# A graph-attention layer on one core: h turned by DMA, v's lo halves behind the second masks, the raise on VectorE, a written-out closing

## The chip, the cores and the metric

The kernel runs on one core of one Trainium2 chip. The metric is the device time in microseconds of that core. Before the change three runs took 616.78, 616.84 and 617.56 us, median 616.84.

## What is computed

x is 32 batches of 256 tokens by 384 features, and adj is a boolean mask of 256 by 256 for each batch. Cut to what matters, the reference is:

```python
h = maximum(layernorm(x), 0.0)
q, k, v = heads(h @ Wq + bq), heads(h @ Wk + bk), heads(h @ Wv + bv)   # 6 heads of 64
scores = einsum('bhqd,bhkd->bhqk', q, k) / sqrt(64)
probs = softmax(scores + where(adj, 0.0, -9e15))
ctx = einsum('bhqk,bhkd->bhqd', probs, v)
out = x + ctx.reshape(32, 256, 384) @ Wf + bf
```

Inputs and outputs are float32. The kernel multiplies in float16 with each operand split into a high and a low half, so that most products are three matmuls: hi by hi, hi by lo, lo by hi.

## The kernel before, in words

Names: B is 32 batches, P is 128, S is 256 tokens in QT = 2 tiles t, C is 3 chunks of 128 features. A unit u (0 to 5) of a batch is a pair of heads j = u % 3 for one query tile t = u // 3. Every engine has its own program, written out by hand, in which the order of the work is fixed; engines meet only at semaphores. All of them go through `cycle(b)` for b = 1 to 33, and `cycle(b)` works on four batches at once: scores and softmax of batch b, the last four units of batch b-1 and its output, the output's second half of batch b-2, and the projections of batch b+1.

For each batch: VectorE takes the moments of x (`layer_stats`, `layer_moments`), GpSimd makes `normed` (`normalise`, L345). TensorE turns `normed` in six float32 transposes (`transpose_h`, L862, matmuls of L874) into PSUM banks ring 0 and ring 1; ScalarE writes the relu of it as `h_hi` (L486), VectorE the rest as `h_lo` (L637). TensorE projects q and k for each pair of heads (`project_qk`, 18 matmuls of 256 columns each) and v for each token tile (`project_v`, 9 matmuls of 384 columns each). ScalarE takes q and k out of PSUM (`qk_full`), VectorE and GpSimd split them; ScalarE writes `v_hi` (L500), VectorE `v_lo` (`v_lo_part`, L650).

`scores(b, g)` (L910) computes two units with 12 matmuls. `mask_and_max(b, u)` (L623) on VectorE adds the mask to the two heads of a unit and keeps the smallest element of each row in `least`; each head is one long instruction and one short one that reads the accumulator out. `exps` (L471) on ScalarE first adds a constant to `least`, giving `raised` (L475), and then takes two exponentials; `probs_hi` on ScalarE and `probs_lo` on GpSimd (L379) split them into `p_rows`. SyncE's queue turns `p_rows` into `p_cols` with one transposing DMA per unit (`transpose_probs`, L271). `apply_probs` (L927) multiplies by v into the bank ctx with 12 matmuls, four units after the scores. `divide` (L657) on VectorE needs three applied units. `transpose_context` (L944, three transposes), `context_hi`, `context_lo` and `project_out` (L955, 9 matmuls of 384 columns) make the output tile, `finish` (L672) adds the residual, and SyncE stores it.

Four PSUM banks are shared as a ring. Bank ring 3 holds v of tile 0 (`R_V[0]`, L154), then the output of tile 1 (`R_OUT[1]`, L156), then q and k of pair 1. So `project_out(b-2, 1)` of `cycle(b)` may overwrite ring 3 only when VectorE has read v of batch b out of it. It says so in its second wait (L957 and L958):

```python
def project_out(b, t):
    wait(pe, ct_lo_ready, b.count(2, t + 1))
    if t == 1 and (b + 2).exists():
        wait(pe, v_lo_ready, (b + 2).count(2, 1))
```

The start of `cycle(b)` before the change is, on TensorE (L1026 to L1034): scores(b, 0), apply_probs(b-1, 2), transpose_h(b+1), project_out(b-2, 1), apply_probs(b-1, 3), project_qk(b+1, 0), scores(b, 1). On VectorE (L803 to L817): mask_and_max(b, 0), divide(b-1, 0), h_lo_part(b+1), mask_and_max(b, 1), v_lo_part(b, 1), finish(b-2, 1). v_lo_part(b, 0) stands at the end of `cycle(b-1)` (L849).

Of the kernel before, what the change touches and what calls it, by code (L numbers as in the profile page):

```python
# [35 lines left out]
P = 128  # L36
# [17 lines left out]
def gnn_attention(nc, x, adj, Wq, bq, Wk, bk, Wv, bv, Wf, bf, out):  # L54
# [11 lines left out]
    with ctx:  # L66
# [23 lines left out]
        p_raise = sb("p_raise", [P, 1], F32)  # L90
# [28 lines left out]
        h_hi = [sb(f"h_hi{p}", [P, C, S], F16) for p in range(2)]  # L119
        h_lo = [sb(f"h_lo{p}", [P, C, S], F16) for p in range(2)]  # L120
# [36 lines left out]
        ctx_ps = ctx_bank[:, 0:HEADS * V1].rearrange("p (h d) -> p h d", h=HEADS)  # L157
# [35 lines left out]
        h_lo_ready = sem("h_lo_ready")  # L193
        qk_ready = sem("qk_ready")
# [11 lines left out]
        p_lo_ready = sem("p_lo_ready")  # L206
        ctx_ready = sem("ctx_ready")
# [32 lines left out]

        def pair(j):

            return slice(j * P, (j + 1) * P)
# [3 lines left out]

        def cycles(cycle):

            for k in range(1, B + 2):  # L250
                cycle(Batch(k))
# [8 lines left out]
        def _(sp):  # L260
# [10 lines left out]
            def transpose_probs(b, u):  # L271
# [3 lines left out]
                                       p_rows[u][:].rearrange("p w a k -> p (w a k)")).then_inc(p_placed[u], 16)  # L275

# [21 lines left out]
            def cycle(b):  # L298
# [20 lines left out]

                if here:  # L320
                    transpose_probs(b, 2)
# [14 lines left out]
            transpose_probs(Batch(0), 3)  # L336
            cycles(cycle)
            for t in range(QT):
                sp.wait_ge(out_stored[t], 16 * (B + 1))
# [3 lines left out]
        def _(pool):  # L343
            def normalise(b):
# [4 lines left out]
                wait(pool, ht_ready, b.count(2, 0))  # L349
# [35 lines left out]
            pool.memset(p_raise[:], P_RAISE).then_inc(pool_const, 1)  # L385
            pool.wait_ge(pool_const, 4)
# [80 lines left out]


        @block.scalar
        def _(act):  # L470
            def exps(b, u):  # L471

                wait(act, p_lo_ready, b.count(UNITS, u - 2))
                wait(act, logits_ready, b.count(2 * UNITS, 2 * u + 2))
                act.activation(raised[u % 3][:], least[u % 3][:], ACT.Identity,  # L475
                               bias=p_raise[:, 0:1]).then_inc(raised_ready, 1)
# [9 lines left out]
            def h_hi_part(b):  # L486
                for n, (c0, c1, src) in enumerate(((0, 2, R_HT[0]), (2, 3, R_HT[1]))):
                    wait(act, ht_ready, b.count(2, n + 1))
                    act.activation(h_hi[b.parity][:, c0:c1].rearrange("p c s -> p (c s)"),  # L489
                                   src[:, 0:(c1 - c0) * S], ACT.Relu).then_inc(h_hi_ready, 1)  # L490

# [32 lines left out]
            act.wait_ge(pool_const, 5)  # L524
# [33 lines left out]
            qk_full(Batch(1), 2)  # L558
            exps(Batch(0), 4)
# [50 lines left out]


# [473 lines left out]
```

## Time and profile before

| | |
|---|---|
| median of three runs | 616.84 us |
| profiled execution, its own time | 617.89 us |
| its span, first to last instruction | 616.0 us |
| mean granted TensorE clock | 0.989 |
| instructions | 18008 |

The profile is of one execution. Its own time is 1.89 us more than its span, and 1.05 us more than the median. Busy time of an engine is the sum over its instructions; matmuls overlap one another in this profile (their ends are modelled), so the distance from one start to the next tells what a matmul costs in a stream.

### The profile page before, as it was taken

The page shows a single profiled execution, that of the slowest core. Times are in us where ns is not written, and L with a number is a line of the kernel's source. Part 1 is how long each engine was busy: PE and PEld are TensorE (multiplying, and loading weights), DVE is VectorE, ACT ScalarE, POOL GpSimd, SP SyncE. Part 2 cuts the span into 40 slices and gives each one's busy share as a digit, 9 for nine tenths or more (in the row PEclk, how much of TensorE's full clock was granted, in tenths as well). Part 3 has the DMA queues.
Part 4 walks back from the last instruction along what each step waited for, and adds up shares of the span by engine and source line. Part 5 has one row for each costly group of instructions (what it writes and reads, how often), then busy time and mean ns, then how long its engine had stood idle before and what let it go on. Part 6 is the DMA issues. An engine that isn't in the chain of part 4 may idle for free.

```text
span 616.0 us, 18008 instructions
## 1 busy us (share of the span) xinstructions
PE 596.3 (97%) x6806; PEld 451.9 (73%) x6806; DVE 456.9 (74%) x1479; ACT 516.5 (84%) x1166; POOL 496.1 (81%) x529
## 2 busy tenths in 40 slices
PE   7998999999999999999999999999999999999975
PEld 7666777777777777777777777777777777777753
DVE  5878777878777777877777787777778777776762
ACT  2688888889888889988888898888889888888980
POOL 2789888888888888888888888888888888888750
PEclk9998999999999999999999999999999999999997
DMA  8056766867766786666578767666886666765573
GB/s 264 6 100 117 133 124 128 157 128 146 139 139 122 129 159 127 145 131 150 118 129 159 130 141 134 142 123 129 159 136 136 140 141 121 126 133 112 100 136 80
DMA packets 232280, 81.14 MB, mean 132 GB/s; under 512 B 214273, under 2 KB 232194, under 8 KB 232194
## 3 DMA queue, kind: packets, MB, share of 16 engines
q1 hardware_dynamic: 230992, 79.99, 66.1%
q8 instruction: 54, 0.88, 0.6%
q14 instruction: 32, 0.26, 0.2%
q10 hardware_dynamic: 1202, 0.01, 0.1%
HBM read 17.05 MB, written 12.58 MB: 48 GB/s over the span
## 4 chain that ended last, share of the span: by engine, by line
PE 87%; ACT 6%; DVE 2%; DMA 2%; issue 1%; POOL 1%; ACTq 0%; DVEq 0%; POOLq 0%
PE ring L858 19%; PE ring L860 19%; PE ring L859 19%; PE scores L922 11%; PE ctx L939 5%; PE ring L951 4%; PE ctx L940 3%; PE ctx L941 3%; PE ring L874 3%; ACT probs L479 2%; DMA bf_row<-in_L_gnn_bf_dram 1%; ACT qk L496 1%; ACT p_rows L484 1%; DMA p_cols<-p_rows 1%; PE ring L981 1%
## 5 line engine op out<-in xcount | busy, mean ns | idle before, releaser
L379 POOL TENSOR_TENSOR p_rows<-probs,p_rows 128x512 f16<-128x512 f32 x192 | 222.4, 1158 | 58.5 <-ACT p_rows L484 57.3
L632 DVE CUSTOM_DVE_ANT_0 logits<-scores,mask,logit_unscale 128x256 f32<-128x256 f32 x384 | 169.1, 477 | 39.0 <-PE scores L922 37.1
L479 ACT ACTIVATE probs<-logits,raised 128x256 f32<-128x256 f32 x384 | 174.3, 500 | 6.2
L858 PE MATMUL ring<-h_hi,w_hi 128*128 128x256 f16 x576 | 157.7, 274 | 0.6 <-DVE h_lo L640 0.6
L860 PE MATMUL ring<-h_hi,w_lo 128*128 128x256 f16 x576 | 157.5, 273 | 0.0
L859 PE MATMUL ring<-h_lo,w_hi 128*128 128x256 f16 x576 | 157.4, 273 | 0.0
L365 POOL TENSOR_TENSOR split<-qk,split 128x512 f16<-128x512 f32 x96 | 111.0, 1157 | 25.2 <-DVE split L648 25.2
L484 ACT ACTIVATE p_rows<-probs 128x512 f16<-128x512 f32 x192 | 121.0, 630 | 6.1
L496 ACT ACTIVATE qk<-ring,qk_bias_s,qkv_ratio 128x256 f32<-128x256 f32 x192 | 96.3, 551 | 3.9 <-PE ring L860 3.9
L939 PE MATMUL ctx<-v_hi,p_cols 128*128 128x65 f16 x768 | 90.7, 196 | 7.4 <-DMA p_cols<-p_rows 4.4
L939 PEld LDWEIGHTS ctx<-v_hi,p_cols 128*128 128x128 f16 x768 | 70.2, 97 | 33.4 <-issue 23.6
L652 DVE SCALAR_TENSOR_TENSOR v_lo<-ring,qkv_ratio,v_hi 128x384 f16<-128x384 f32 x64 | 39.5, 618 | 70.6 <-ACT v_hi L502 70.6
L940 PE MATMUL ctx<-v_lo,p_cols 128*128 128x64 f16 x768 | 90.1, 193 | 0.0
L941 PE MATMUL ctx<-v_hi,p_cols 128*128 128x65 f16 x768 | 89.7, 194 | 0.0
L922 PE MATMUL scores<-split 64*128 64x256 f16 x1152 | 80.2, 272 | 3.1 <-DVE least L632 2.2
L940 PEld LDWEIGHTS ctx<-v_lo,p_cols 128*128 128x128 f16 x768 | 71.2, 99 | 4.2
L922 PEld LDWEIGHTS scores<-split 64*128 64x128 f16 x1152 | 48.8, 94 | 31.2 <-issue 24.7
L941 PEld LDWEIGHTS ctx<-v_hi,p_cols 128*128 128x128 f16 x768 | 71.5, 98 | 0.0
L374 POOL TENSOR_TENSOR residual<-x_in,bf_full 128x384 f32<-128x384 f32 x64 | 68.3, 1087 | 0.0
L648 DVE CAST split<-qk 128x512 f16<-128x512 f32 x96 | 55.6, 579 | 14.1 <-ACT qk L496 12.1
L489 ACT ACTIVATE h_hi<-ring 128x512 f16<-128x512 f32 x64 | 27.9, 487 | 45.0 <-PE ring L874 45.0
L858 PE MATMUL ring<-w_hi,ct_hi 128*128 128x384 f16 x192 | 63.3, 329 | 1.7 <-DVE ct_lo L668 1.7
(89 smaller groups left out, 1222.2 us busy)
## 6 DMA issues: line engine op xcount, KB each, us to landing
x_in<-in_x_dram SPq DMA_DIRECT2D x32, 384.0 KB, 3.9
out_dram<-result SPq DMA_DIRECT2D x64, 192.0 KB, 2.2
p_cols<-p_rows SPq DMA_TRANSPOSE x192, 3.1
adj_in<-in_adj_dram SPq DMA_DIRECT2D x32, 64.0 KB, 2.6
w_raw<-in_L_gnn_Wq_dram SPq DMA_DIRECT2D x1, 576.0 KB, 5.8
w_raw<-in_L_gnn_Wv_dram SPq DMA_DIRECT2D x1, 576.0 KB, 7.9
w_raw<-in_L_gnn_Wf_dram SPq DMA_DIRECT2D x1, 576.0 KB, 9.1
w_raw<-in_L_gnn_Wk_dram SPq DMA_DIRECT2D x1, 384.0 KB, 6.8
```

The lines of the kernel that those rows point to most:

```text
L365: pool.tensor_tensor(split[b.parity][j][:, 0:4:3, :], qk32[j][:], split[b.parity][j][:, 1:3, :], ALU.subtract).then_inc(qk_lo_ready, 1)
L379: pool.tensor_tensor(p_rows[u][:, 1], probs[u % 3][:], p_rows[u][:, 0], ALU.subtract).then_inc(p_lo_ready, 1)
L479: act.activation(probs[u % 3][:, a], logits[u % 3][:, a], ACT.Exp, bias=raised[u % 3][:, a:a + 1], scale=-1.0).then_inc(probs_ready, 1)
L484: act.activation(p_rows[u][:, 0], probs[u % 3][:], ACT.Copy).then_inc(p_hi_ready, 1)
L632: dve.tensor_tensor_reduce(out=logits[u % 3][:, a], in0=score_bank[a][:, u % 2 * S:(u % 2 + 1) * S], in1=mask[b.parity][:, t], scale=logit ...
L858: pe.matmul(out_ap, a_hi, m_hi, start=first, stop=False)
L859: pe.matmul(out_ap, a_hi, m_lo, start=False, stop=False)
L860: return pe.matmul(out_ap, a_lo, m_hi, start=False, stop=last)
L922: mm = pe.matmul(score_bank[a][:, u % 2 * S:(u % 2 + 1) * S], tile[own, q, t * P:(t + 1) * P], tile[own, k], start=(n == 0), stop=(n == 2))
L939: pe.matmul(ctx_ps[:, h], hi, vh, start=(s == 0), stop=False)
L940: pe.matmul(ctx_ps[:, h, 0:D], hi, vl, start=False, stop=False)
L941: mm = pe.matmul(ctx_ps[:, h], lo, vh, start=False, stop=(s == QT - 1))
```

## The change

It has these parts.

- Batches 2 to 31: `normed` is no longer turned by TensorE. ScalarE writes its relu in float16 as it lies (`h_hi_rows`, two instructions), VectorE the rest (`h_lo_rows`, two instructions), and one transposing DMA of SyncE's queue per batch turns both halves into `h_cols`. In `cycle(b)` this is done for batch b+2. Batches 0 and 1 stay with TensorE. The waits by which ring 0 and ring 1 were kept for those transposes move to `project_qk`.
- v_lo_part(b, 0) moves from the end of `cycle(b-1)` to `cycle(b)`, behind mask_and_max(b, 1) and directly ahead of v_lo_part(b, 1). `project_out` is not changed.
- `raised` is made by VectorE at the end of every mask_and_max, after a wait for its own `least`, instead of by ScalarE.
- The cycles end with b = 30. What cycles 31 to 33 did is written out for every engine: units 4 and 5 of the last batch are turned by TensorE, the last batch's first context goes to the bank peaks, its second tile is divided, turned and projected in two parts (four heads, two heads), and its result is written to `normed`.

The diff, cut to its core:

```diff
+
+        h_rows = sb("h_rows", [P, 2, C, QT, P], F16)
+        h_cols = [sb(f"h_cols{p}", [P, 2, C, S], F16) for p in range(2)]
...
+        LAST, PREV = Batch(B - 1), Batch(B - 2)
+        last_pt = {4: ring[2], 5: score_bank[0]}
+        UP_TO, FROM = slice(0, 2), slice(2, 3)
+
+        def ctx_of(b, t):
+
+            bank = peak_bank if b.k == B - 1 and t == 0 else ctx_bank
+            return bank[:, 0:HEADS * V1].rearrange("p (h d) -> p h d", h=HEADS)
...
+        BY_PE = 2
+
         def cycles(cycle):
 
-            for k in range(1, B + 2):
+            for k in range(1, B - 1):
                 cycle(Batch(k))
...
+            def transpose_h(b):
+
+                wait(sp, h_lo_ready, b.count(2, 2))
+                sp.dma_start_transpose(h_cols[b.parity][:].rearrange("p w c (t k) -> p (w c t) k", k=P),
+                                       h_rows[:].rearrange("p w c t n -> p (w c t n)")).then_inc(h_placed, 16)
...
+                if (b + 2).exists():
+                    transpose_h(b + 2)
                 if here:
                     transpose_probs(b, 2)
...
+            transpose_h(Batch(2))
             cycles(cycle)
...
-                wait(pool, ht_ready, b.count(2, 0))
+                wait(pool, ht_ready if b.k <= BY_PE else h_lo_ready, b.count(2, 0))
...
+            probs_lo(PREV, 5)
+            probs_lo(LAST, 0)
+            probs_lo(LAST, 1)
+            probs_lo(LAST, 2)
+            probs_lo(LAST, 3)
...
                 wait(act, p_lo_ready, b.count(UNITS, u - 2))
-                wait(act, logits_ready, b.count(2 * UNITS, 2 * u + 2))
-                act.activation(raised[u % 3][:], least[u % 3][:], ACT.Identity,
-                               bias=p_raise[:, 0:1]).then_inc(raised_ready, 1)
                 wait(act, raised_ready, b.count(UNITS, u + 1))
                 for a in range(2):
...
+            def h_hi_rows(b):
+
+                wait(act, h_placed, (b.k - BY_PE) * 16)
+                for t in range(QT):
+                    wait(act, norm_ready, b.count(2, t + 1))
+                    act.activation(h_rows[:, 0, :, t], normed[:, t].rearrange("p (c n) -> p c n", n=P),
+                                   ACT.Relu).then_inc(h_hi_ready, 1)
...
-                if front:
-                    h_hi_part(b + 1)
...
+                if (b + 2).exists():
+                    h_hi_rows(b + 2)
                 if before:
...
+            def turned_hi(u, nth):
+
+                act.wait_ge(pt_ready, nth)
+                act.activation(p_cols[u][:, 0].rearrange("p a s q -> p (a s q)"), last_pt[u][:],
+                               ACT.Copy).then_inc(pt_hi_ready, 1)
...
+            exps(LAST, 0)
+            probs_hi(LAST, 0)
+            v_hi_part(LAST, 1)
+            exps(LAST, 1)
+            probs_hi(LAST, 1)
+            exps(LAST, 2)
+            probs_hi(LAST, 2)
+            context_hi(PREV, 0)
+            exps(LAST, 3)
+            probs_hi(LAST, 3)
+            exps(LAST, 4)
+            exps(LAST, 5)
+            turned_hi(4, 1)
+            context_hi(PREV, 1)
+            turned_hi(5, 2)
+            context_hi(LAST, 0)
+            context_hi_last(UP_TO, 2)
+            context_hi_last(FROM, 3)
...
+                dve.wait_ge(logits_ready, b.count(2 * UNITS, 2 * u + 2))
+                dve.tensor_scalar(raised[u % 3][:], least[u % 3][:], P_RAISE, None, ALU.add).then_inc(raised_ready, 1)
...
+            def h_lo_rows(b):
+
+                for t in range(QT):
+                    wait(dve, h_hi_ready, b.count(2, t + 1))
+                    dve.scalar_tensor_tensor(
+                        out=h_rows[:, 1, :, t], in0=normed[:, t].rearrange("p (c n) -> p c n", n=P),
+                        scalar=0.0, in1=h_rows[:, 0, :, t], op0=ALU.max, op1=ALU.subtract).then_inc(h_lo_ready, 1)
...
+            h_lo_rows(Batch(2))
             layer_stats(Batch(3), (1,))
             layer_moments(Batch(3))
-            v_lo_part(Batch(1), 0)
...
-                if front:
-                    h_lo_part(b + 1)
 
                 if here:
                     mask_and_max(b, 1)
                 if here:
+                    v_lo_part(b, 0)
                     v_lo_part(b, 1)
...
+                if (b + 2).exists():
+                    h_lo_rows(b + 2)
...
                     finish(b + -1, 0)
                     context_lo(b + -1, 1)
-                if front:
-                    v_lo_part(b + 1, 0)
 
             cycles(cycle)
...
+            def turned_lo(u, nth):
+
+                dve.wait_ge(pt_hi_ready, nth)
+                dve.tensor_tensor(p_cols[u][:, 1].rearrange("p a s q -> p (a s q)"), last_pt[u][:],
+                                  p_cols[u][:, 0].rearrange("p a s q -> p (a s q)"),
+                                  ALU.subtract).then_inc(pt_lo_ready, 1)
...
+            def divide_last(chunks, units, nth):
+
+                h = slice(2 * chunks.start, 2 * chunks.stop)
+                ctx_ps = ctx_of(LAST, 1)
+                dve.wait_ge(ctx_ready, LAST.count(UNITS, units))
+                dve.reciprocal(inv_sum[1][:, h], ctx_ps[:, h, D]).then_inc(inv_ready, 1)
+                dve.wait_ge(inv_ready, LAST.count(2, nth))
+                dve.tensor_tensor(context[1][:, h], ctx_ps[:, h, 0:D],
+                                  inv_sum[1][:, h].unsqueeze(2).to_broadcast([P, h.stop - h.start, D]),
...
+            mask_and_max(LAST, 0)
+            mask_and_max(LAST, 1)
+            divide(PREV, 0)
+            v_lo_part(LAST, 0)
+            v_lo_part(LAST, 1)
+            mask_and_max(LAST, 2)
+            mask_and_max(LAST, 3)
+            finish(PREV + -1, 1)
+            context_lo(PREV, 0)
+            mask_and_max(LAST, 4)
+            mask_and_max(LAST, 5)
+            divide(PREV, 1)
+            finish(PREV, 0)
+            turned_lo(4, 1)
+            context_lo(PREV, 1)
+            divide(LAST, 0)
+            turned_lo(5, 2)
+            finish(PREV, 1)
+            divide_last(UP_TO, 5, 2)
+            context_lo(LAST, 0)
+            context_lo_last(UP_TO, 2)
+            divide_last(FROM, 6, 3)
+            context_lo_last(FROM, 3)
+            finish_last(0)
+            finish_last(1)
 
 
...
-                    if (b + -3).exists():
-                        if n == 0:
-                            wait(pe, ct_lo_ready, (b + -3).count(2, 2))
-                        else:
-                            wait(pe, result_ready, (b + -3).count(2, 1))
...
-                if j == 0:
+                if j == 0 and b.k < BY_PE:
                     wait(pe, h_lo_ready, b.count(2, 2))
+                elif j == 0:
+                    wait(pe, h_placed, (b.k - BY_PE + 1) * 16)
+                if j == 0 and (b + -3).exists():
+                    wait(pe, ct_lo_ready, (b + -3).count(2, 2))
...
-                wait(pe, p_placed[u], b.count(16, 16))
+                ctx_ps = ctx_of(b, t)
+                if b.k == B - 1 and u >= 4:
+                    pe.wait_ge(pt_lo_ready, u - 3)
+                else:
+                    wait(pe, p_placed[u], b.count(16, 16))
                 if u == 0:
                     wait(pe, v_lo_ready, b.count(2, 2))
-                if j == 0:
+                if b.k == B - 1 and u == C:
+                    pe.wait_ge(context_ready, b.count(2, 0))
+                elif j == 0 and b.k != B - 1:
...
                 attend(0)
-                if front:
-                    transpose_h(b + 1)
                 if (b + -2).exists():
                     project_out(b + -2, 1)
...
+            def turn_probs(u):
+
+                if u == 4:
+                    pe.wait_ge(v_lo_ready, LAST.count(2, 2))
+                else:
+                    pe.wait_ge(logits_ready, LAST.count(2 * UNITS, 2 * UNITS))
+                for a in range(2):
+                    pe.wait_ge(probs_ready, LAST.count(2 * UNITS, 2 * u + a + 1))
+                    for n in range(QT):
+                        o = (a * QT + n) * P
+                        mm = pe.transpose(last_pt[u][:, o:o + P], probs[u % 3][:, a, n * P:(n + 1) * P], ident[:])
+                mm.then_inc(pt_ready, 1)
...
+            scores(LAST, 0)
+            apply_probs(PREV, 2)
+            project_out(PREV + -1, 1)
+            apply_probs(PREV, 3)
+            scores(LAST, 1)
+            transpose_context(PREV, 0)
+            apply_probs(PREV, 4)
+            scores(LAST, 2)
+            apply_probs(PREV, 5)
+            project_out(PREV, 0)
+            apply_probs(LAST, 0)
+            transpose_context(PREV, 1)
+            turn_probs(4)
+            apply_probs(LAST, 1)
+            turn_probs(5)
+            apply_probs(LAST, 2)
+            project_out(PREV, 1)
+            transpose_context(LAST, 0)
+            apply_probs(LAST, 3)
+            apply_probs(LAST, 4)
+            transpose_context_last(UP_TO, 2)
+            apply_probs(LAST, 5)
+            project_out(LAST, 0)
+            project_out_last(UP_TO, 2)
+            transpose_context_last(FROM, 3)
+            project_out_last(FROM, 3)
```

## Rows read from the trace of the kernel before

**Rows 1.** The page: busy time (share of the span) and instructions of the engines
```profile
PE 596.3 (97%) x6806; PEld 451.9 (73%) x6806; DVE 456.9 (74%) x1479; ACT 516.5 (84%) x1166; POOL 496.1 (81%) x529
```

**Rows 2.** The page: the chain that ended last, by engine
```profile
PE 87%; ACT 6%; DVE 2%; DMA 2%; issue 1%; POOL 1%; ACTq 0%; DVEq 0%; POOLq 0%
```

**Rows 3.** The chain in order of time, one cycle in the middle: start us, us, what
```profile
298.99 0.76 PE scores L922 x12
...
300.21 0.69 PE ring L874 x6
...
301.06 0.16 PE ring L859
...
316.91 0.76 PE scores L922 x12
```

**Rows 4.** Instructions of PE in time, start of that cycle: start us, us, what
```profile
298.92 0.83 PE L922 MATMUL scores<-split 64*128 64x256 f16 x12
...
300.02 0.20 PE L941 MATMUL ctx<-v_hi,p_cols 128*128 128x65 f16 x1
...
300.74 0.33 PE L858 MATMUL ring<-w_hi,ct_hi 128*128 128x384 f16 x1
...
304.63 0.83 PE L922 MATMUL scores<-split 64*128 64x256 f16 x12
```

**Rows 5.** Instructions of DVE in time, same cycle; in brackets idle time and its releaser
```profile
299.37 0.62 DVE L652 SCALAR_TENSOR_TENSOR v_lo<-ring,qkv_ratio,v_hi 128x384 f16<-128x384 f32 x1 [1.64 <-ACT v_hi L502]
299.90 0.47 DVE L632 CUSTOM_DVE_ANT_0 logits<-scores,mask,logit_unscale 128x256 f32<-128x256 f32 x1
...
300.71 0.08 DVE L632 DVE_READ_ACCUMULATOR2_ANT least<- 128x1 f32 x1
300.71 0.19 DVE L660 RECIPROCAL inv_sum<-ctx 128x6 f32<-128x6 f32 x1
300.93 0.56 DVE L662 TENSOR_TENSOR context<-ctx,inv_sum 128x384 f32<-128x384 f32 x1
301.41 1.01 DVE L640 SCALAR_TENSOR_TENSOR h_lo<-ring,h_hi 128x512 f16<-128x512 f32 x2
...
305.50 0.48 DVE L632 CUSTOM_DVE_ANT_0 logits<-scores,mask,logit_unscale 128x256 f32<-128x256 f32 x1 [0.48 <-PE scores L922]
```

**Rows 6.** Groups of instructions by form: busy us, mean ns | idle before
```profile
L697 DVE TENSOR_SCALAR neg_mean<-mean_var 128x2 f32<-128x2 f32 x32 | 5.8, 180 | 0.1
```

**Rows 7.** Busy time in stretches; behind POOL's: granted clock, DMA share, GB/s
```profile
45.50:48.40 2.90, 0.00 (x0) 0.03 (x1) 2.23 (x8) 2.87 (x7) 2.90 (x3) 1.00 0.43 82
50.20:53.60 3.40, 3.40 (x23) 1.97 (x21) 2.90 (x2) 2.80 (x7) 3.40 (x5) 0.50 0.68 93
53.60:57.00 3.40, 3.40 (x50) 3.06 (x49) 2.92 (x11) 2.30 (x6) 2.71 (x4) 1.00 0.85 200
600.90:603.80 2.90, 0.00 (x0) 0.00 (x0) 0.26 (x1) 0.00 (x0) 0.18 (x1) 0.89 1.12 155
603.20:610.00 6.80, 5.64 (x39) 3.81 (x39) 1.57 (x4) 0.49 (x1) 0.00 (x0) 0.50 0.19 50
591.90:593.70 1.80, 0.00 (x0) 0.00 (x0) 1.58 (x8) 1.74 (x6) 1.15 (x1) 1.00 0.97 216
```

**Rows 8.** The chain in order of time, the end: start us, us, what
```profile
598.94 4.86 DMA p_cols<-p_rows
...
607.37 0.32 PE ring L860
...
613.04 0.62 DVE result L677
```

**Rows 9.** Instructions of PE in time: the last batch's first scores
```profile
585.80 0.83 PE L922 MATMUL scores<-split 64*128 64x256 f16 x12
```

**Rows 10.** The page: DMA queues and issues (KB each where known, us to landing)
```profile
q1 hardware_dynamic: 230992, 79.99, 66.1%
...
p_cols<-p_rows SPq DMA_TRANSPOSE x192, 3.1
```

More of the change, by code:

```diff
@@ L206, in gnn_attention @@
         p_lo_ready = sem("p_lo_ready")
+        pt_ready = sem("pt_ready")
+        pt_hi_ready = sem("pt_hi_ready")
+        pt_lo_ready = sem("pt_lo_ready")
         ctx_ready = sem("ctx_ready")
@@ L336, in _, with store_last @@
             transpose_probs(Batch(0), 3)
+            transpose_h(Batch(2))
             cycles(cycle)
+            def store_last(t):
+                sp.wait_ge(result_ready, LAST.count(2, t + 1))
+                sp.dma_start(out_v[LAST.k, t], normed[:, t]).then_inc(out_stored[t], 16)
+            transpose_probs(PREV, 4)
+            store(PREV + -1, 0)
+            transpose_probs(PREV, 5)
+            transpose_probs(LAST, 0)
+            store(PREV + -1, 1)
+            for u in (1, 2, 3):
+                transpose_probs(LAST, u)
+            store(PREV, 0)
+            store(PREV, 1)
+            store_last(0)
+            store_last(1)
             for t in range(QT):
@@ L558, in _ @@
             qk_full(Batch(1), 2)
+            h_hi_rows(Batch(2))
             exps(Batch(0), 4)
@@ new lines, in context_lo_last, with finish_last @@
+            def context_lo_last(chunks, nth):
+                dve.wait_ge(ct_hi_ready, LAST.count(2, nth))
+                dve.tensor_tensor(ct_lo[1][:, chunks].rearrange("p c q -> p (c q)"),
+                                  R_CT[1][:, chunks.start * P:chunks.stop * P],
+                                  ct_hi[1][:, chunks].rearrange("p c q -> p (c q)"),
+                                  ALU.subtract).then_inc(ct_lo_ready, 1)
+            def finish_last(t):
+                dve.wait_ge(out_ready, LAST.count(2, t + 1))
+                dve.wait_ge(residual_ready, LAST.count(2, t + 1))
+                dve.scalar_tensor_tensor(out=normed[:, t], in0=R_OUT[t][:, 0:H], scalar=out_unscale[:, 0:1],
+                                         in1=residual[LAST.slot][:, t], op0=ALU.mult,
+                                         op1=ALU.add).then_inc(result_ready, 1)
@@ new lines, in transpose_context_last, with project_out_last @@
+            def transpose_context_last(chunks, nth):
+                pe.wait_ge(context_ready, LAST.count(2, nth))
+                for c in range(chunks.start, chunks.stop):
+                    mm = pe.transpose(R_CT[1][:, c * P:(c + 1) * P],
+                                      context[1][:, 2 * c:2 * c + 2].rearrange("p h d -> p (h d)"), ident[:])
+                mm.then_inc(ct_ready, 1)
+            def project_out_last(chunks, nth):
+                pe.wait_ge(ct_lo_ready, LAST.count(2, nth))
+                for c in range(chunks.start, chunks.stop):
+                    mm = three(R_OUT[1][:, 0:H], ct_hi[1][:, c], ct_lo[1][:, c],
+                               w_hi[:, 3, c], w_lo[:, 3, c], c == 0, c == C - 1)
+                if chunks.stop == C:
+                    mm.then_inc(out_ready, 1)
```

28 lines of the change are left out of this document (15 added, 13 removed).

## The prediction, made before the changed kernel was run

> **What bounds the kernel now.** I read the page's busy times first: PE is busy for 97% of the span, the next engine for 84% [rows 1]. Busy alone proves little, so I went on to the chain that ended last: 87% of it lies on PE, 6% on ACT, 2% on DVE [rows 2]. In order of time the chain repeats itself: scores(b, 0) starts at 298.99 and again at 316.91 [rows 3]. A cycle takes 17.92 us, and between these rows the chain never leaves PE. So in the steady cycles TensorE alone sets the time: taking matmuls off it gains what they take, and a new wait on it costs its full length. A wait elsewhere costs nothing until TensorE waits for it.
>
> **Part 1, six transposes fewer per cycle.** In the chain they take 0.69 us [rows 3]; by starts, from the last matmul ahead of them at 300.02 to the first behind at 300.74, it is 0.72 us less the 0.03 us of that last matmul [rows 4]. Cycles 1 to 29 and the prologue lose them, 30 times 0.69, some 20 us, if nothing takes their place. The other engines' share: ScalarE and VectorE do two instructions each for h as before, of similar size, in another place. The transposing DMA carries one and a half times the data of one for a unit, which lands in 3.1 us; the queue keeps the DMA engines busy for 66% of the span with six per cycle [rows 10]. Half as much again of one, once per cycle, adds about a fifth of the transposing work, and its reader, project_qk of the next cycle, starts more than 10 us after it is issued. SyncE's queue is passed by no one: units 2 and 3 stand behind it, and they are needed only in the next cycle. I cost this DMA at nothing; if that cover were gone it would be one landing of some 4.6 us (3.1 times 1.5) in a cycle.
>
> **Part 2, v's lo halves behind the second masks.** This is the part that decides. project_out(b-2, 1) is the third thing that TensorE does in cycle b, and it waits until v_lo_part(b, 0) has read bank ring 3 (L958). Before, VectorE did that at the end of cycle b-1; it ended at 299.37 + 0.62 = 299.99 [rows 5], and TensorE came to project_out at 300.74 [rows 4]: the wait was never felt. After, VectorE comes to it only after mask_and_max(b, 0), divide(b-1, 0) and mask_and_max(b, 1), and the first of these needs scores(b, 0), which TensorE has only just computed. TensorE has 12 small matmuls to fill that time and then stands.
>
> Its length, counted from the start s of scores(b, 0):
> - the scores reach VectorE at s + 0.87: 304.63 to 305.50, a start that waited for nothing else [rows 4, 5];
> - a mask_and_max takes 0.81 to the second read of the accumulator (299.90 to 300.71) and 0.08 for the read [rows 5]. The raise waits for it: 0.03 for the wait, as between the reciprocal and the product (0.22 from start to start against 0.19), and 0.18 for an instruction on 128x2 [rows 5, 6], of which 0.04 overlaps the next. Together 1.06, twice 2.12;
> - divide takes 0.22 + 0.48 = 0.70 (300.71 to 300.93 to 301.41), v_lo 0.62 [rows 5], and the step to TensorE about 0.05.
>
> So project_out starts at s + 0.87 + 2.12 + 0.70 + 0.62 + 0.05 = s + 4.36. Before it started at s + 1.82 (298.92 to 300.74 [rows 4]), the transposes included. Each cycle grows by **2.54 us net**, part 1 already taken off. TensorE's last matmul ahead of the wait starts at s + 1.10 (298.92 to 300.02 [rows 4]) and ends 0.20 later, so it is idle for 3.06 us. Cycles 2 to 30 have this wait: 29 x 2.54 = 73.7 us. Cycle 1 has no project_out of tile 1 and gains 0.6. What else waits on TensorE moves with it: behind the VectorE wait stand v_lo_part(b, 1), finish(b-2, 1) and mask_and_max(b, 2); the last has until scores(b, 1), 3.9 us after project_out's start. I take bounds of 2.3 and 2.9 us for the net growth: the lower if the wait and the overlap of the raise cost nothing (2 x 0.11 less), the upper if the raise costs a full 0.18 and waits twice as long, and VectorE starts a little late.
>
> **Part 3, the clock.** Pauses of TensorE of this length are in the trace. Idle from 45.5 to 48.4, it is at 0.50 of full speed, the 1.2 GHz level, in the whole of 50.20 to 53.60. Idle from 600.9 to 603.8, it is at 0.50 from 603.20 to 610.0. Idle from 591.9 to 593.7, 1.8 us, it keeps 1.00 [rows 7]. The new pause, 3.06 us, is of the kind that was followed by the lower level twice out of twice. At that level a matmul of 384 columns takes 0.32 us instead of 0.16 [rows 8, 3]. A low stretch of 3.4 us filled with matmuls loses 1.7 us. Some pauses may escape, and of some the low stretch may fall partly into the pause, so I take **1.5 us per pause**, 30 pauses (the closing has one too), 45 us. Bounds: nothing, and 1.7 for each; 3.4 us if all were like that at 603.2, which also had further pauses behind it.
>
> The Trainium skill, "TensorE: Matmul & The Clock Gate", section "Why this matters for your kernels", says the same of pauses between bursts of matmuls, that one of enough idleness puts the clock back to its half, and speaks thereby against this change. By it the sum is the one with this term, 730; without it, it would be 685.
>
> **Part 4, the raise.** ScalarE is rid of six small instructions per cycle. It is not on the chain, so this is worth nothing; on VectorE they cost the two raises counted above, and four more between waits for scores, where the DVE row shows idle time (0.48 ahead of 305.50 [rows 5]).
>
> **Part 5, the closing.** From the last batch's scores(31, 0) at 585.80 [rows 9] to the end of the span it was 30.2 us. Its chain ends with unit 5's transposing DMA of 4.86 us, a run of half-speed matmuls, and the result [rows 8]. After, by the order written out: project_out(29, 1) at +4.4 (the same wait), the masks of units 2 and 3 done at +9.2, scores 2 to +10.0, masks and exponentials of 4 and 5 to +13.3, unit 5 turned at +13.9, then unit 2, project_out (9 x 0.163 = 1.46), context and units 3 and 4 to +17.0, divide and transposes to +18.1, unit 5, nine and six matmuls to +20.9, the last two heads to +22.7, result and store to +25.7. It saves about **4.5 us** against 30.2, with its own wait inside and its clock in part 3. Bounds: 0 and 8.
>
> **Sum.** 617.9 (the profiled execution) + 73.7 + 45 - 0.6 - 4.5 = 731.5; the median is 1.05 below the profiled execution, so 730.4 for a median. I say 730.
>
> **The rivals.**
> - Wait without clock. The pause of 1.8 us kept the clock [rows 7], and the new one has dense work on both sides. Then 616.8 + 73.7 - 5.1 = 685. Against it: both pauses of 2.9 us lost the clock. With few drops it is between 685 and 710.
> - Longer low stretches, as the one of 6.8 us at 603.2: 29 x (2.5 + 2.5) and more, 760 or above. Against it: behind this pause stand several microseconds of unbroken matmuls, and after 50.2 such work had the full clock back by 53.6 [rows 7].
> - Faster: the new wait isn't felt and only the transposes go. This is decided at one place, project_out(b-2, 1), and by whether v_lo_part(b, 0) ends before s + 1.13. It would give 616.8 - 20 - 4.5 = 592. It needs VectorE to pass that read ahead of the masks; the order of its program excludes this, and the two masks alone take longer. Only if I misread the count of that semaphore does it come about.
> - The change doesn't do what it says: the DMA turn of h may be late. It would only lengthen the same cycle, since the wait for h stands behind the pause.
>
> **How the numbers follow.** Wait with the clock falling in most cycles: 0.74, 715 to 750. Wait with few or no drops: 0.17, 683 to 714. Longer than 750: 0.05. Faster, near 592: 0.03. No change: 0.01, a sum that happens to cancel. The predicted time is the first case's, 730. The range of 8 in 10 takes in the first case and the second down to the wait alone: 684 to 750. A measurement of this kernel can tell about 0.2% from no change, 1.2 us. Faster by over that 0.03, within it 0.01, slower by over it 0.96.
>
> **What would show it.** In the changed profile: an idle time of about 3.1 us ahead of project_out's first matmul or weight load, released by VectorE's v_lo, 30 times; the cycle from scores to scores at 20.5 us where the clock stays, 22 where it falls; granted clock near 0.85 in the middle of the span; no transposes of normed after batch 1; PE's busy share down to about 85%; the chain passing through DVE's masks in every cycle. The forecast is wrong if cycles are shorter than 17.9 us (the wait isn't there), if the pause is much shorter than 3 us (the raise or the masks are cheaper), or if the pauses are there and the clock stays at 1.00.

## The result, and the profile after

| | before | changed |
|---|---|---|
| median | 616.97 us | 789.01 us |
| all runs | 616.78 to 617.56 | 788.58 to 790.21 |
| ratio | 1 | 1.279 (95% interval 1.277 to 1.281) |
| span of the profiled execution | 616.0 us | 787.5 us |
| mean granted TensorE clock | 0.989 | 0.867 |

The median before is of four runs here, one more than ahead of the prediction. The change makes the kernel 28% slower. The forecast was slower, with a range of 684 to 750 us; the time lies 39 us above it. The page of the changed kernel, its busy times and its chain by engine, beside [rows 1] and [rows 2]:

```profile
PE 643.2 (82%) x6634; PEld 462.6 (59%) x6634; DVE 573.2 (73%) x1676; ACT 471.5 (60%) x975; POOL 506.3 (64%) x526
...
DVE 47%; PE 31%; ACT 11%; issue 9%; DMA 1%; POOL 1%; ACTq 0%; DVEq 0%; POOLq 0%
```

No engine is busy for more than 82% now, and DVE holds 47% of the chain, where it was 2%: the engines wait on one another in turn. Who waited for whom (us in total, times, longest us):

```profile
PE ring L1012 <- DVE v_lo L746: 126.4, 30, 4.6
```

That is the wait that was forecast, 30 times, in its place: L1012 is the first matmul of `project_out(b-2, 1)`. But in 27 of the 30 it is 4.3 us long, not 3.06. Instructions of PE in one cycle (start us, us, what; in brackets idle time and its releaser), to be read against [rows 4]:

```profile
400.46 0.83 PE L1075 MATMUL scores<-split 64*128 64x256 f16 x12
...
401.56 0.20 PE L1100 MATMUL ctx<-v_hi,p_cols 128*128 128x65 f16 x1
...
406.04 0.48 PE L1012 MATMUL ring<-w_hi,ct_hi 128*128 128x384 f16 x1 [4.29 <-DVE v_lo L746]
```

From the scores' start, project_out starts at +5.58, where the prediction had +4.36. The same stretch on DVE, against [rows 5]:

```profile
401.33 0.48 DVE L716 CUSTOM_DVE_ANT_0 logits<-scores,mask,logit_unscale 128x256 f32<-128x256 f32 x1
...
402.26 1.05 DVE L721 TENSOR_SCALAR raised<-least 128x2 f32<-128x2 f32 x1
403.22 0.18 DVE L755 RECIPROCAL inv_sum<-ctx 128x6 f32<-128x6 f32 x1
403.44 0.56 DVE L757 TENSOR_TENSOR context<-ctx,inv_sum 128x384 f32<-128x384 f32 x1
403.91 0.47 DVE L716 CUSTOM_DVE_ANT_0 logits<-scores,mask,logit_unscale 128x256 f32<-128x256 f32 x1
...
404.83 0.55 DVE L721 TENSOR_SCALAR raised<-least 128x2 f32<-128x2 f32 x1
405.29 1.13 DVE L746 SCALAR_TENSOR_TENSOR v_lo<-ring,qkv_ratio,v_hi 128x384 f16<-128x384 f32 x2
...
413.94 0.17 DVE L721 TENSOR_SCALAR raised<-least 128x2 f32<-128x2 f32 x1
```

Everything is as forecast but the raise: of the 1.22 us by which project_out comes later than forecast, 1.15 lie in the two raises. An instruction on two elements per partition takes 1.05 and 0.55 us in this chain, and 0.17 at 413.94. The instructions of POOL in that time tell why:

```profile
402.13 1.15 POOL L421 TENSOR_TENSOR p_rows<-probs,p_rows 128x512 f16<-128x512 f32 x1 [0.65 <-ACT p_rows L528]
...
404.05 1.31 POOL L393 TENSOR_SCALAR normed<-x_in,neg_mean,rstd 128x384 f32<-128x384 f32 x2
...
407.37 1.15 POOL L421 TENSOR_TENSOR p_rows<-probs,p_rows 128x512 f16<-128x512 f32 x1
414.51 1.16 POOL L407 TENSOR_TENSOR split<-qk,split 128x512 f16<-128x512 f32 x1 [5.99 <-DVE split L742]
```

The first raise ends at 402.26 + 1.05 = 403.31, GpSimd's p_rows at 402.13 + 1.15 = 403.28. The second ends at 404.83 + 0.55 = 405.38, GpSimd's second normed at 404.05 + 1.31 = 405.36. At 413.94 GpSimd is idle, from 408.52 to 414.51. So the raise lasts until the instruction that GpSimd is in has ended. The whole trace holds to this: all 122 raises (of 192) that took more than 0.25 us end 0.02 to 0.03 us after an instruction of GpSimd, and none of the shorter ones began inside one that went on.

Busy time in stretches (the number behind POOL's is the granted clock), against [rows 7]:

```profile
401.80:403.80 2.00, 0.00 (x0) 0.00 (x0) 1.93 (x7) 1.12 (x3) 1.67 (x2) 1.00 0.86 209
404.00:410.50 6.50, 4.46 (x26) 2.71 (x27) 3.00 (x8) 2.95 (x6) 4.47 (x6) 0.50 0.42 81
410.80:424.40 13.60, 13.60 (x156) 10.20 (x156) 11.12 (x35) 8.95 (x20) 8.43 (x8) 1.00 0.62 132
```

The clock falls to its lower level, 1.2 GHz, within the pause and is up again at about 410.6, after 4.5 us of matmuls at half speed: a low stretch of at least 6.5 us, about twice the 3.4 that the prediction took as usual. project_out follows project_out after 23.89 us, in 27 cycles one after the other (23.86 to 23.91). The growth of 23.89 - 17.92 = 5.97 us, 29 times, is 173 us: the whole loss of 172. VectorE has no slack left either: from 413.01 on it works without a pause, and it is free for the next first mask only as the scores arrive. That is why so much of the chain runs over DVE.

### The profile page after: what moved, and what is told of

It is laid out like the page before. It is cut to its first block, busy times and chain, and to the rows that moved or that the text cites. A ratio compares the mean times of both kernels' runs of the same rounds, so it can differ in the third digit from the quotient of the medians.

```text
span 787.5 us, 17725 instructions
## 1 busy us (share of the span) xinstructions
PE 643.2 (82%) x6634; PEld 462.6 (59%) x6634; DVE 573.2 (73%) x1676; ACT 471.5 (60%) x975; POOL 506.3 (64%) x526
## 4 chain that ended last, share of the span: by engine, by line
DVE 47%; PE 31%; ACT 11%; issue 9%; DMA 1%; POOL 1%; ACTq 0%; DVEq 0%; POOLq 0%
DVE logits L716 16%; DVE raised L721 11%; PE ring L1012 9%; PE ring L1013 8%; PE ring L1014 8%; DVE h_rows L735 6%; ACT probs L523 4%; DVE stats L781 3%; DVE split L742 3%; ACT h_rows L541 3%; ACT qk L548 2%; DVE result L772 2%; DVE v_lo L746 2%; DVE ct_lo L763 2%; ACT ct_hi L559 1%
## 5 line engine op out<-in xcount | busy, mean ns | idle before, releaser
L421 POOL TENSOR_TENSOR p_rows<-probs,p_rows 128x512 f16<-128x512 f32 x190 | 231.6, 1219 | 38.5 <-ACT p_rows L528 38.5
L1012 PE MATMUL ring<-w_hi,ct_hi 128*128 128x384 f16 x192 | 79.2, 413 | 128.3 <-DVE v_lo L746 126.4
L1012 PE MATMUL ring<-h_cols,w_hi 128*128 128x256 f16 x576 | 166.1, 288 | 0.5 <-DMA h_cols<-h_rows 0.5
L1013 PE MATMUL ring<-h_cols,w_hi 128*128 128x256 f16 x576 | 165.8, 288 | 0.0
L1014 PE MATMUL ring<-h_cols,w_lo 128*128 128x256 f16 x576 | 162.9, 283 | 0.0
L721 DVE TENSOR_SCALAR raised<-least 128x2 f32<-128x2 f32 x192 | 126.6, 659 | 6.6
L1012 PEld LDWEIGHTS ring<-w_hi,ct_hi 128*128 128x128 f16 x192 | 22.1, 115 | 146.3 <-issue 139.5
L1098 PE MATMUL ctx<-v_hi,p_cols 128*128 128x65 f16 x756 | 96.9, 204 | 3.5 <-DVE context L757 3.5
L1100 PE MATMUL ctx<-v_hi,p_cols 128*128 128x65 f16 x756 | 95.6, 201 | 0.0
L772 DVE SCALAR_TENSOR_TENSOR result<-ring,out_unscale,residual 128x384 f32<-128x384 f32 x62 | 37.9, 611 | 78.7 <-PE ring L1014 78.7
L1014 PE MATMUL ring<-w_hi,ct_lo 128*128 128x384 f16 x192 | 80.6, 420 | 0.0
L1013 PE MATMUL ring<-w_lo,ct_hi 128*128 128x384 f16 x192 | 80.6, 420 | 0.0
```

The lines of the kernel that those rows point to most:

```text
L421: pool.tensor_tensor(p_rows[u][:, 1], probs[u % 3][:], p_rows[u][:, 0], ALU.subtract).then_inc(p_lo_ready, 1)
L721: dve.tensor_scalar(raised[u % 3][:], least[u % 3][:], P_RAISE, None, ALU.add).then_inc(raised_ready, 1)
L1012: pe.matmul(out_ap, a_hi, m_hi, start=first, stop=False)
L1013: pe.matmul(out_ap, a_hi, m_lo, start=False, stop=False)
L1014: return pe.matmul(out_ap, a_lo, m_hi, start=False, stop=last)
L1098: pe.matmul(ctx_ps[:, h], hi, vh, start=(s == 0), stop=False)
```

## The experiments

Each kernel differs from the changed one (or, where said, from the one before) by the edit shown. The kernel before ran beside them on the same chip at 615.5 to 616.3 us; ratios are to it. All diffs are cut.

**v_back.** v's read goes back to its old place.

```diff
                 if here:
-                    v_lo_part(b, 0)
                     v_lo_part(b, 1)
...
                     context_lo(b + -1, 1)
+                if front:
+                    v_lo_part(b + 1, 0)
```

> The changed kernel, with v_lo_part(b, 0) put back to the end of the cycle before (and the prologue and closing to match). Theory: TensorE's wait in project_out(b-2, 1) for v's lo half makes the loss; without it a cycle is again 17.9 us or less and the time falls from 789 to between 592 and 625 us: 592 if TensorE bounds it (6 transposes of 0.69 us less per cycle), up to 625 if the six raises on VectorE, 0.66 us each on average, make VectorE the bound (its busy time in the changed kernel is 573 us in 32 batches, 17.9 us each). Rival: the DMA turn of h or the raise makes the loss: 740 us or more stay.

651.05 us, ratio 1.057 (1.054 to 1.059). So 138 of the 172 us hang on the place of v's read. But 651 is above the range given, and the wait has not gone:

```profile
300.52 0.32 PE L1013 MATMUL ring<-w_hi,ct_hi 128*128 128x384 f16 x1 [1.58 <-DVE v_lo L746]
319.74 0.32 PE L1013 MATMUL ring<-w_hi,ct_hi 128*128 128x384 f16 x1 [1.58 <-DVE v_lo L746]
```

A cycle takes 19.2 us, with 1.58 us of it waiting for the same read. With the raise on ScalarE as well (both_back, below) that wait is 0.9 us at most and the time 614.57: it is the raises that make the read late here, and they cost 36 us.

**raise_act.** The raise goes back to ScalarE, v's read stays behind the second masks.

```diff
+                wait(act, logits_ready, b.count(2 * UNITS, 2 * u + 2))
+                act.activation(raised[u % 3][:], least[u % 3][:], ACT.Identity,
+                               bias=p_raise[:, 0:1]).then_inc(raised_ready, 1)
                 wait(act, raised_ready, b.count(UNITS, u + 1))
...
-                dve.wait_ge(logits_ready, b.count(2 * UNITS, 2 * u + 2))
-                dve.tensor_scalar(raised[u % 3][:], least[u % 3][:], P_RAISE, None, ALU.add).then_inc(raised_ready, 1)
```

> The changed kernel, with the raise put back to ScalarE; v's lo half stays behind the second masks. Theory: the chain from scores(b, 0) to project_out loses two raises (1.05 and 0.55 us in the trace) and their waits, so the pause of TensorE falls from 4.3 to about 2.6 us and the cycle by 1.7 us: 737 us if the clock still falls after a pause of 2.6 us, 675 if it doesn't. Rival, the raise is cheap and only stretched in the record: 780 us or more.

691.83 us, ratio 1.126 (1.119 to 1.132), between the two values expected, since the clock falls in only every third cycle for most of the run:

```profile
294.25 0.32 PE L1015 MATMUL ring<-w_hi,ct_hi 128*128 128x384 f16 x1 [2.65 <-DVE v_lo L749]
314.31 0.48 PE L1015 MATMUL ring<-w_hi,ct_hi 128*128 128x384 f16 x1 [2.66 <-DVE v_lo L749]
335.65 0.32 PE L1015 MATMUL ring<-w_hi,ct_hi 128*128 128x384 f16 x1 [2.65 <-DVE v_lo L749]
355.71 0.32 PE L1015 MATMUL ring<-w_hi,ct_hi 128*128 128x384 f16 x1 [2.66 <-DVE v_lo L749]
```

The pause is 2.65 us as expected. Cycles take 20.06 us, and 21.34 where the first matmul is stretched to 0.48 us, a sign that the clock is already low.

**both_back.** Both edits together; h by DMA and the closing are left.

> The changed kernel with both put back: v's lo half at the end of the cycle before and the raise on ScalarE. What is left of the change is h turned by DMA and the written-out closing. If TensorE bounds it, 30 times 0.69 us and about 4 us of closing go: 592 us. If the DMA turn of h or its two instructions on VectorE hold anything up, more, up to 617 us.

614.57 us, ratio 0.998 (0.996 to 0.999). Three ways of undoing give 138, 97 and 174 us. Counted from this kernel the raise alone costs 36 us and the place of v's read alone 77, both together 174: each makes the other worse, and together they are the whole loss. Against the expectation of 592 the TensorE time saved didn't come back as time. The cycle takes 18.05 us. Its chain by engine, and its waits (us in total, times, longest), of which the last is a small rest of the same kind:

```profile
ACT 60%; DVE 17%; issue 14%; PE 6%; DMA 2%; POOL 1%; ACTq 0%; POOLq 0%; DVEq 0%
...
DVE v_lo L749 <- ACT v_hi L559: 76.5, 62, 1.7
...
PE ring L1016 <- DVE v_lo L749: 17.6, 29, 0.9
```

v's read waits for ScalarE's v_hi, the first mask stands behind it on VectorE, and ScalarE in turn waits for the mask. TensorE holds 6% of the chain and ScalarE 60%: this loop, and no longer TensorE, sets the 18.05 us.

**raise_psum.** The raise stays on VectorE and behind its wait; only its form changes (batches 1 to 30). Its second input is two columns of the PSUM bank peaks, set to zero once.

```diff
-                dve.tensor_scalar(raised[u % 3][:], least[u % 3][:], P_RAISE, None, ALU.add).then_inc(raised_ready, 1)
...
+                    dve.scalar_tensor_tensor(out=raised[u % 3][:], in0=least[u % 3][:], scalar=P_RAISE,
+                                             in1=peak_bank[:, 510:512], op0=ALU.add,
+                                             op1=ALU.add).then_inc(raised_ready, 1)
```

> The changed kernel, with the raise still on VectorE and behind the same wait, but (batches 1 to 30) as an instruction whose second input is a zero in PSUM. If the 0.66 us mean of a raise is a wait for GpSimd's instruction to end that comes from the raise's form (both tensors in SBUF, one source), it falls to about 0.2 us here and the time to some 750 us (two raises on the chain, 1.2 us less per cycle, clock as before). If the time belongs to the wait for its own least or to the place in the order, the raise stays at 0.6 us and the time at 789 us.

697.18 us, ratio 1.131 (1.129 to 1.134): 92 us from the form of one small instruction, and 53 less than the 750 expected, which had the clock falling as before. Durations in ns, least, median and most, first of the changed kernel, then of this run:

```profile
L721 DVE TENSOR_SCALAR raised<-least x192: 168/548/1178, 27.4 to 772.5; 128x2 f32<-128x2 f32 x192
```

```profile
L722 DVE SCALAR_TENSOR_TENSOR raised<-least,peaks x180: 156/156/157, 47.8 to 661.4; 128x2 f32<-128x2 f32 x180
...
292.09 0.83 PE L1082 MATMUL scores<-split 64*128 64x256 f16 x12
...
296.42 0.32 PE L1019 MATMUL ring<-w_hi,ct_hi 128*128 128x384 f16 x1 [3.03 <-DVE v_lo L752]
...
316.85 0.32 PE L1019 MATMUL ring<-w_hi,ct_hi 128*128 128x384 f16 x1 [3.03 <-DVE v_lo L752]
```

With one input in PSUM no raise waits, though some 85 of the 180 begin inside an instruction of GpSimd that goes on. The name of the instruction is not what frees it: h_rows is a SCALAR_TENSOR_TENSOR too, with both inputs in SBUF, and is stretched (run reordered). This is also the kernel that the prediction had priced: project_out at 296.42 - 292.09 = +4.33 (forecast +4.36), a pause of 3.03 us (3.06), a cycle of 20.43 us (20.46). What is missing to 730 is the clock, which fell in only 3 of 29 cycles (and behind the closing's pause). The Trainium skill, "SBUF — State Buffer", section "SBUF: two separate sides", says that VectorE and GpSimd hold a shared pair of SBUF ports as an exclusive lock for a whole instruction, and that a VectorE instruction in a two-port mode needs it, or one with two SBUF inputs while GpSimd's reads SBUF. The rows agree: raises end with GpSimd's instruction, and the one with a PSUM input doesn't wait. That the raise of the change ran in a two-port mode, no row here shows.

**clock_fill.** 18 matmuls that nobody reads fill most of the pause.

```diff
                 if (b + -2).exists():
+                    for _ in range(18):
+                        pe.matmul(peak_bank[:, 0:H], w_hi[:, 0, 0, 0:P], w_hi[:, 0, 1], start=True, stop=True)
                     project_out(b + -2, 1)
```

> The changed kernel with 18 idle-time matmuls (128x384 float16, about 2.9 us in all, into a bank that nothing reads) on TensorE ahead of project_out(b-2, 1) in cycles 2 to 30, inside the pause of 4.28 us. They do no useful work. If the clock's fall after that pause costs what the trace says (23.89 us per cycle against 17.92 + 2.54 + 1.2 for the wait alone = 21.7), the clock stays at 1.00 and the time falls from 789 to about 725 us though more work is done. If the clock is not part of the loss, the time stays at 789 us or rises.

725.33 us, ratio 1.179 (1.177 to 1.182), where 725 was expected: more work, 64 us less time.

```profile
310.66 0.32 PE L1012 MATMUL ring<-w_hi,ct_hi 128*128 128x384 f16 x1 [1.36 <-DVE v_lo L746]
332.35 0.32 PE L1012 MATMUL ring<-w_hi,ct_hi 128*128 128x384 f16 x1 [1.37 <-DVE v_lo L746]
```

The mean granted clock is 0.992, a cycle takes 21.69 us, and 23.89 - 21.69 = 2.20 us is what the clock's fall cost in each.

**reordered.** raise_psum with two moves.

```diff
                     mask_and_max(b, 0)
+                if here:
+                    v_lo_part(b, 0)
...
                 if here:
-                    v_lo_part(b, 0)
                     v_lo_part(b, 1)
...
+                if front:
+                    project_qk(b + 1, 0)
                 if (b + -2).exists():
                     project_out(b + -2, 1)
...
                 attend(1)
-                if front:
-                    project_qk(b + 1, 0)
```

> The changed kernel with three edits: the raise in the form with a zero in PSUM (0.16 us), v_lo_part(b, 0) on VectorE directly behind mask_and_max(b, 0), and on TensorE project_qk(b+1, 0) ahead of project_out(b-2, 1), so that 1.97 us of matmuls cover the wait. Theory: all of the loss came from the place of the v_lo read and the cost of the raise; with both repaired TensorE bounds the cycle at 17.92 - 0.69 = 17.2 us and the time is 592 us. Rival: another loop (ScalarE to VectorE and back, which gave 18.05 us per cycle with both put back) holds it at 610 us or more.

631.18 us, ratio 1.024 (1.020 to 1.028): a miss. The wait for v's read is gone, and another has taken its place. First PE, then DVE and POOL ahead of it:

```profile
320.22 0.83 PE L1083 MATMUL scores<-split 64*128 64x256 f16 x12 [0.96 <-DVE least L716]
...
315.19 1.05 DVE L748 CAST split<-qk 128x512 f16<-128x512 f32 x1
...
316.75 2.60 DVE L741 SCALAR_TENSOR_TENSOR h_rows<-normed,h_rows 128x384 f16<-128x384 f32 x2
...
316.32 1.16 POOL L407 TENSOR_TENSOR split<-qk,split 128x512 f16<-128x512 f32 x1 [0.36 <-DVE split L748]
317.78 1.16 POOL L421 TENSOR_TENSOR p_rows<-probs,p_rows 128x512 f16<-128x512 f32 x1 [0.30 <-ACT p_rows L528]
```

The two h_rows instructions have both inputs in SBUF and take 2.60 us, where one takes 0.54 at the least; the cast takes 1.05 us, where 0.42 is the least. They too wait for GpSimd: the second h_rows ends at 319.35, 0.41 us after GpSimd's p_rows (317.78 + 1.16), and so do all 58 stretched ones of the 60, each 0.41 to 0.42 us after an instruction of GpSimd. VectorE is 88% busy, and the cycle takes 18.47 us.

**v_alone.** The kernel before, with v's read behind the second masks and nothing else.

> The kernel before with one part of the change: v_lo_part(b, 0) behind mask_and_max(b, 1) in cycle b. The raise stays on ScalarE, h on TensorE. From scores(b, 0): 0.87, two masks 1.62, divide 0.70, h_lo_part 0.93, v_lo 0.62 and 0.05, so project_out starts at +4.8 instead of +1.8: a cycle of 20.9 us, 703 us without a fall of the clock, up to 765 with one in every cycle. If the move alone is harmless, 617 us.

Four runs: 765.66, 790.21, 790.90 and 791.12 us, too far apart for an interval. The first has the profile, and it shows cycles of three kinds, with the same pause:

```profile
155.31 0.32 PE L856 MATMUL ring<-w_hi,ct_hi 128*128 128x384 f16 x1 [2.95 <-DVE v_lo L652]
177.99 0.32 PE L856 MATMUL ring<-w_hi,ct_hi 128*128 128x384 f16 x1 [2.95 <-DVE v_lo L652]
199.03 0.32 PE L856 MATMUL ring<-w_hi,ct_hi 128*128 128x384 f16 x1 [2.95 <-DVE v_lo L652]
...
331.32 0.48 PE L856 MATMUL ring<-w_hi,ct_hi 128*128 128x384 f16 x1 [2.95 <-DVE v_lo L652]
355.17 0.48 PE L856 MATMUL ring<-w_hi,ct_hi 128*128 128x384 f16 x1 [2.95 <-DVE v_lo L652]
```

A cycle takes 21.04 us without a fall of the clock (20.9 expected), 22.68 with a short low stretch behind the pause and 23.85 with a longer one. The granted clock in the first of these cycles, behind a first matmul that is not stretched:

```profile
156.30:159.50 3.20, 3.20 (x24) 2.23 (x23) 0.62 (x1) 0.74 (x2) 1.84 (x3) 0.50 0.58 130
```

From 90 to 306 us the clock falls so in every third cycle, and from there on in every one. The three longer runs have a mean granted clock of 0.866 to 0.868, against 0.902, which fits a fall in every cycle from the start; they have no trace. With 2.8 us for each of 29 falls, the 703 expected without a fall becomes 784, and not 765. In this kernel the h transposes and h_lo_part lengthen the way, so that the move alone can cost as much as the whole change.

**raise_alone.** The kernel before, with the raise on VectorE and nothing else.

> The kernel before with one part of the change: the raise on VectorE, in the form of the change. If it waits for GpSimd's instructions (0.66 us on average, six per cycle, 4 us on top of 14.3 us busy), VectorE comes to 18.3 us per cycle and TensorE waits for it: 630 to 660 us. If a raise costs its 0.17 us, nothing changes: 617 us or a little less, since ScalarE is relieved.

647.42 us, ratio 1.052 (1.050 to 1.055), inside the range: the raise costs 32 us by itself. DVE holds 32% of the chain, where it held 2% before.

**reordered_act.** reordered, with the raise on ScalarE.

> As the run reordered, but with the raise on ScalarE as in the kernel before. In that run VectorE held the cycle at 18.47 us: it was 88% busy, and scores(b, 2) waited 0.96 us for its masks, behind two h_rows instructions of 2.60 us in all and a cast of 1.05 us. Without six raises and their waits (0.27 us each, 1.6 us per cycle) VectorE has room, and v's read no longer stands between ScalarE and the first mask, as it did with both put back (18.05 us per cycle). If that loop was the bound there, the cycle falls to about 17.3 us and the time to some 595 us. If VectorE's stretched instructions hold this one too, 610 us or more.

596.40 us, ratio 0.969 (0.966 to 0.972). This is faster than both kernels.

```profile
PE 573.9 (97%) x6634; PEld 434.5 (73%) x6634; DVE 478.8 (81%) x1484; ACT 518.1 (87%) x1167; POOL 492.1 (83%) x527
...
PE 90%; DVE 4%; ACT 2%; DMA 2%; issue 1%; POOL 1%; ACTq 0%; DVEq 0%; POOLq 0%
...
301.06 0.82 PE scores L1079 x12
...
318.37 0.82 PE scores L1079 x12
```

TensorE is 97% busy again and holds 90% of the chain; a cycle takes 17.31 us.

**reordered_act_h.** h_lo_rows moves behind divide(b-1, 1), its DMA behind that of unit 2.

> As reordered_act, and h_lo_rows on VectorE moves from ahead of mask_and_max(b, 3) to behind divide(b-1, 1), with its DMA on SyncE's queue behind that of unit 2. scores(b, 2) then waits for less on VectorE. If that place holds the cycle, this is faster than reordered_act by up to 0.5 us per cycle, 15 us; if TensorE is the bound there, the two agree within 2 us, near 595 us.

597.36 us, ratio 0.970 (0.967 to 0.973), the same as reordered_act within the intervals. TensorE is the bound there; h_lo_rows holds nothing up.

**closing_only.** The kernel before with the written-out closing.

> The kernel before with the change's written-out closing and nothing else of it (h on TensorE, v's read and the raise where they were). By the working of the prediction the closing saves 4.5 us: 612 us beside 616. If units 4 and 5 on TensorE only take the place of the DMA's wait, 616 us. What both_back (0.998 of the kernel before) has beyond this is what h's turn by DMA brings or costs by itself.

612.23 us, ratio 0.994 (0.991 to 0.996): 3.3 us saved; the interval takes in the 4.5. So turning h by DMA gave nothing that can be told with both parts back (614.57). From 612.2 down to the 596.4 of reordered_act are some 16 us, for h's turn and the two moves together: no run has the new order with the transposes on TensorE.

**v_first_act.** reordered_act, with TensorE's order of the change.

> As reordered_act, but with TensorE's order as in the change: project_out(b-2, 1) stands right behind apply_probs(b-1, 2) again. v's read is now behind the first mask only. From scores(b, 0): 0.87, one mask 0.81, v_lo 0.62 and 0.05 give project_out's start at +2.35, where TensorE is there at +1.13: a wait of 1.2 us, too short for the clock to fall, a cycle of 17.2 + 1.2 = 18.4 us and a time of 630 us. If the wait is covered or another loop decides, 597 us as in reordered_act.

631.89 us, ratio 1.025 (1.023 to 1.027), and the wait as worked out:

```profile
307.51 0.32 PE L1016 MATMUL ring<-w_hi,ct_hi 128*128 128x384 f16 x1 [1.15 <-DVE v_lo L749]
```

A wait behind one mask still costs 35 us against reordered_act: moving v's read alone is not enough. Whether moving project_qk alone would be, no run shows.

## Why the prediction was wrong

**Part 2, the wait, was right in place and mechanism, and one term was mis-sized.** The failing step is "the raise waits for it: 0.03 for the wait ... and 0.18 for an instruction on 128x2 ... Together 1.06, twice 2.12". The 0.18 came from L697 [rows 6], a mean over 32 instructions. In the trace before, 31 of them took 0.154 to 0.163 us and one 0.866, and that one stands in GpSimd's time:

```profile
L697 DVE TENSOR_SCALAR neg_mean<-mean_var x32: 154/158/866, 6.2 to 546.8; 128x2 f32<-128x2 f32 x32
...
115.98 0.87 DVE L697 TENSOR_SCALAR neg_mean<-mean_var 128x2 f32<-128x2 f32 x1
...
114.68 2.15 POOL L374 TENSOR_TENSOR residual<-x_in,bf_full 128x384 f32<-128x384 f32 x2
```

It ends at 116.85, GpSimd's residual at 116.83. On this chain the two raises take 1.05 and 0.55 us, since GpSimd is in p_rows (1.15 us) and then in the second of two normed (1.31 us together). That puts project_out at +5.58 instead of +4.36, 1.22 us per cycle. The bounds given, 2.3 to 2.9 us of net growth, missed the 3.76. With the raise at 0.156 us (raise_psum) the rest of the sum holds to 0.03 us. So the warning was in the very row that the prediction used, had it been read by its largest member and not by its mean. The cast of q and k, also one SBUF source, gave it too: 0.42 to 1.14 us before.

**Part 3, the clock, was right that it falls and wrong in size.** I took 1.5 us per pause of 3.06 us, from a low stretch of 3.4 us. With the real pause of 4.3 us the clock fell every time, stayed low for at least 6.5 us and cost 2.20 us (clock_fill). That is the clock of the rival "longer low stretches", 760 or above, to which I had given 0.05; the argument against it, that unbroken matmuls stand behind the pause, did not hold. At the pause that I had forecast the clock fell in 3 of 29 cycles (raise_psum). "Twice out of twice" was too thin: it held for two pauses ringed by other waits, and the rival "wait without clock", 683 to 714 us, at 0.17, is what raise_psum measured, 697. So the 45 us for the clock were too little for this kernel and too much for the one that I had priced: the clock's cost hung on the pause, and I had taken the two as separate terms.

**The sum.** 1.22 + (2.20 - 1.5) = 1.92 us per cycle, 29 times, is 56 us; 730 + 56 = 786 against 789. By the cycle: 3.76 us for the wait and 2.20 for the clock, of the 5.97 measured.

**Part 1** was right for what was looked at: the transposes left TensorE, and h's DMA (3.8 us to landing, 4.6 estimated) was late for nobody in the steady cycles. I costed h's instructions on VectorE as of similar size; they are stretched to 1.08 us in the median against 0.54 at the least, which the changed kernel hides, if only just, and which decided in reordered. The gain of some 20 us was said to come only "if nothing takes their place"; both_back shows that ScalarE's loop with VectorE would have taken it even without the wait. At 18.05 us that loop lies just above the 17.92 of TensorE before, so TensorE's 87% of the chain did not mean that there was room under it.

**Part 4** missed the same wait for GpSimd: six raises cost 32 us alone, through VectorE (raise_alone). That they are "worth nothing" on ScalarE no run tests by itself.

**Part 5**: the closing took 787.5 - 758.3 = 29.2 us from the last batch's first scores, where 30.2 - 4.5 = 25.7 was forecast, with its own pause of 3.10 us and a low clock; in the order before it saves 3.3 us (closing_only), within the bounds of 0 and 8.

**The faster rival**, with the new wait not felt, was excluded rightly.

## What to carry to other kernels

When a read that frees a buffer moves behind other work, find who waits for the buffer and where that wait stands in its own order; the cost is the distance between the two, in every cycle. Price a small VectorE instruction not by its mean elsewhere but by what GpSimd is doing at its new place, and look at the largest member of a group as well as at its mean: with its data in SBUF it can last until GpSimd's instruction ends, and one operand in PSUM avoided that here. A pause of TensorE costs more than its length if the clock falls, and moving independent matmuls into it, as with project_qk in reordered_act, can repair both.

## What the runs showed of the hardware

- A raise on 128x2 float32 took 0.168 to 1.178 us, the long ones all ending with an instruction of GpSimd; with its second input in PSUM, 0.156 to 0.157 us in all 180 cases.
- Whether the clock falls isn't decided by the pause's length alone. A pause of 4.3 us dropped it in every cycle; of 3.03 us in 3 of 29; of 2.65 us in every third for most of the run; of 2.95 us (v_alone) in every third cycle up to 306 us and in every cycle later in the same run. Why is left open. Pauses of 1.15 us (v_first_act), 1.4 us with matmuls ahead of it (clock_fill) and 1.58 us (v_back) never did.
- A fall cost 1.3 us per cycle in raise_act, 2.20 in the changed kernel, 1.6 and 2.8 in v_alone.
- Useless matmuls in a pause made the kernel 64 us faster.
